# Quantising and the first product by whole batches of 256 tokens, with x1 formed in place

## What is computed

```python
# L0: 8 thresholds, deltas, zero points
gi = sum(abs(x)[..., None] <= thresholds, -1);  idx = min(gi, G - 1)
d, zp = deltas[idx], zero_points[idx]
q = where(gi == G, 0, (clip(round(x / d) + zp, 0, 63) - zp) * d)
x = x + q                                        # x1
x = x + einsum('bsi,boi->bso', x, W1[id_a[b]])   # x2, a 1024 x 1024 matrix per batch
x = x + x @ W2.T + 0.5 * (x @ A[id_b[b]]) @ B_w.T
x = x + ((x @ B3[id_a[b]].T) @ A3[id_a[b]].T)
```

## Time and profile before

| | us |
|---|---|
| median of 3 runs | 483.82 |
| the 3 runs | 483.77, 483.82, 486.87 |
| profiled execution, first to last instruction | 481.9 |

### The profile page before, as it was taken

The page is one execution under the profiler, slowest core; times in us unless marked ns, Lnnn a source line. Parts: engine busy times, 40 slices in busy tenths (PEclk is TensorE's granted clock), DMA queues, the critical chain, the costliest instruction groups (busy, mean ns, idle before and its releaser), DMA issues.

```text
span 481.9 us, 8215 instructions
## 1 busy us (share of the span) xinstructions
PE 464.9 (96%) x3184; PEld 424.7 (88%) x3184; DVE 419.4 (87%) x481; ACT 358.6 (74%) x383; POOL 45.5 (9%) x46
## 2 busy tenths in 40 slices
PE   3999869999999999999999999999999999999997
PEld 3969669898999989898999989898999989898995
DVE  5999999999999899989999899989999899989120
ACT  6979958678877879678877879678887879675011
POOL 1064000200002000200002000210003000100000
PEclk9999989999999999999999999999999999999999
DMA  7997214712335122712335122712335122702002
GB/s 282 407 415 258 113 34 149 294 54 97 131 127 212 44 95 97 294 44 103 131 120 218 44 89 101 294 44 103 131 101 237 44 86 104 294 2 88 1 1 87
DMA packets 17830, 67.07 MB, mean 139 GB/s; under 512 B 2576, under 2 KB 5904, under 8 KB 13712
## 3 DMA queue, kind: packets, MB, share of 16 engines
q1 hardware_dynamic: 17808, 66.81, 37.9%
HBM read 56.84 MB, written 9.96 MB: 139 GB/s over the span
## 4 chain that ended last, share of the span: by engine, by line
PE 90%; ACT 3%; DMA 3%; DVE 2%; issue 1%; POOL 1%; SPq 0%; DVEq 0%
PE x_bank L603 45%; PE acc L628 34%; PE acc L579 3%; PE x_bank L616 3%; PE acc L640 2%; PE acc L638 2%; DMA w1b<-w 2%; DMA rows<-own_rows 1%; ACT mask L344 1%; ACT w2h L400 1%; DVE y L460 1%; PE acc L567 1%; ACT tq L329 1%; PE acc L577 0%; ACT outb L404 0%
## 5 line engine op out<-in xcount | busy, mean ns | idle before, releaser
L603 PEld LDWEIGHTS x_bank<-x,w1b 128*128 128x128 f32 x2048 | 233.2, 193 | 8.2 <-issue 4.9
L603 PE MATMUL x_bank<-x,w1b 128*128 128x128 f32 x2048 | 234.8, 276 | 3.7 <-DVE x L475 3.7
L344 ACT ACTIVATE mask<-absx,negtop 128x1024 bf16<-128x1024 f32 x112 | 128.4, 1146 | 40.3 <-DVE y L460 39.5
L329 ACT ACTIVATE tq<-xin,magic,rdelta 128x1024 f32<-128x1024 f32 x128 | 157.0, 1234 | 0.6 <-DVE yhigh L526 0.3
L460 DVE COPY_PREDICATED y<-mask,uq 128x1024 f32<-128x1024 int16 x112 | 151.1, 1349 | 0.1
L439 DVE TENSOR_SCALAR tq<-tq,par 128x1024 f32<-128x1024 f32 x128 | 99.2, 775 | 3.7 <-DVE y L460 3.1
L448 DVE TENSOR_SCALAR uq<-tq,ylow,yhigh 128x1024 f32<-128x1024 f32 x112 | 92.3, 824 | 0.2 <-DVE y L460 0.2
L628 PE MATMUL acc<-w2h,x2h 128*128 128x512 f32 x256 | 80.9, 393 | 2.0 <-DVE x2l L481 2.0
L628 PE MATMUL acc<-w2h,x2l 128*128 128x512 f32 x256 | 79.9, 390 | 0.0
L628 PE MATMUL acc<-w2l,x2h 128*128 128x512 f32 x256 | 79.2, 390 | 0.0
L295 POOL TENSOR_TENSOR w1b<-w1b,eye 128x256 f32<-128x256 f32 x32 | 36.5, 1140 | 368.9 <-DMA w1b<-w 368.9
(11 more groups left out here) (57 smaller groups left out, 218.9 us busy)
## 6 DMA issues: line engine op xcount, KB each, us to landing
w1b<-w SPq DMA_DIRECT2D x32, 1024.0 KB, 6.7
xin<-x SPq DMA_DIRECT2D x16, 512.0 KB, 3.7
out<-outb SPq DMA_DIRECT2D x14, 512.0 KB, 2.8
w1b<-w2n SPq DMA_DIRECT2D x4, 1024.0 KB, 10.6
ring<-w2t SPq DMA_DIRECT2D x6, 512.0 KB, 6.7
ua<-e_dram SPq DMA_DIRECT2D x16, 128.0 KB, 2.5
ua<-w2t SPq DMA_DIRECT2D x2, 512.0 KB, 7.8
va<-la SPq DMA_DIRECT2D x8, 128.0 KB, 2.7
```

What stands on the lines that cost most here:

```text
L329: nc.scalar.activation(tq[:, n % TQ, :], flat(xin, c % UN), ACT.Identity, bias=magic[:, 0:1], scale=rdelta[:, g:g + 1]).then_inc(t_ready, 1)
L344: nc.scalar.activation(mask[:, n % MK, :], absx[:, :], ACT.Relu, bias=negtop[:, g:g + 1], scale=1.0).then_inc(mask_ready, 1)
L603: last = nc.tensor.matmul(x2_bank[2 * t + i][:, o % HALF * P:(o % HALF + 1) * P], w1b[:, o, at:at + P], x1[:, t, k, :], start=(o % HALF == ...
```

## The change

- **Quantising by batch.** A step is now a batch and a group: 64 steps of 2048 elements per partition in place of 128 of 1024. Each `multiple`, `exceeds`, `value`, `clamp`, `select` and both closing operations have twice the width and half the count. `clamp` writes back into `tq`, and `uq` is gone; a tq buffer is free only when its `select` is done, and there are 3 in place of 4.
- **x1 in place.** `xin` and `x1` become `xs`, two slots of a whole batch; x1 of a batch is written over its x. x(b+2) is loaded when W1 of batch b is done. Batch 0's x comes in two halves of 512 KB, and both come ahead of the tables' inputs; its first |x|, `multiple` and `value` work by halves.
- **W1 with 256 moving columns.** `w1_x1` runs once a batch over both units: 64 products of 256 columns in place of 128 of 128. x2 is rounded and split in two halves of 1024 elements.
- **PE's order.** W1 of the whole batch, with `u_low` of the last batch after three tiles as before; then the products by W2 for k = 0 to 3 of both units; then k = 4 to 7 of unit 0, v_x2, k = 4 to 7 of unit 1. Batch 0 has the same order and waits for each W2 tile as it goes.
- **Places in the lists.** DVE splits the halves of x2 of batch b at steps 4 and 7 of the quantising of batch b + 1 (2 and 5 for batch 0), the second ahead of that step's `select`. W2 is split at steps 8 to 13, after the first batch is closed. SP issues W2 tiles 4 to 7 behind the stores of the tables, and SP's loop is written out.

The diff, cut to its core (declarations, renamed semaphores and the host's layout of x are left out):

```diff
     P = 128
-    B, _, UN, KT, _ = x.shape
-    T = UN * P
+    B, _, KT, T = x.shape
+    UN = T // P
...
     MAGIC = 1.5 * 2.0 ** 23
     PAIRS = OT // 2
     DH = D // 2
     ACCS = 2 * UN
...
+    TQ, MK, ST = 3, 2, 4
     ctx = ExitStack()
     with ctx:
         def sem(name):
             return ctx.enter_context(nc.semaphore(name))
-        def flat(t, c):
...
-        x2l = sb("x2l", [P, UN, KT, P], f32r)
+        def flat(t):
+            return t.rearrange("p k t -> p (k t)")
+        xs = sb("xs", [P, 2, KT, T])
+        x2h = sb("x2h", [P, KT, T], f32r)
+        x2l = sb("x2l", [P, KT, T], f32r)
...
-        uq = sb("uq", [P, 2, CH])
...
+        b3s = flat(xs[:, 1, 0:HALF, :]).rearrange("p (k r) -> p k r", k=KT)
+        gsb = flat(xs[:, 1, HALF:KT, :]).rearrange("p (a k r) -> p a k r", a=NA, k=KT)
...
+        x2p = ctx.enter_context(nc.psum_tensor("x2p", [P, BANKS, 512], f32))
...
+        low_bank = x2p[:, 3, :]
...
-            load_x(0, 0)
+            load_first(0)
             sp.dma_start(par[:, :, :], params[:, :, :]).then_inc(par_in, 16)
+            load_first(1)
...
-            load_x(0, 1)
...
-            sp.wait_ge(x1_ready, 1)
-            load_x(1, 0)
-            load_w2(4)
-            load_w2(5)
             sp.wait_ge(g_out, 16)
+            load_x(1)
...
-            load_w2(6)
-            load_w2(7)
...
+            for k in range(ST, KT):
+                load_w2(k)
             sp.wait_ge(e_out, 16 * EH)
             sp.wait_ge(w2l_ready, ST + 1)
             load_u(a0)
...
+            for b in range(LAST):
                 a, lab = ids_of(b + 1)
-                if not first:
+                if b:
                     store(b - 1, 0)
                     store(b - 1, 1)
-                sp.wait_ge(vl_ready, 2 * (b + 1))
-                load_v(a, lab)
-                sp.wait_ge(x1_ready, UN * b + 2)
-                load_x(b + 1, 1)
                 for j in range(PAIRS):
                     sp.wait_ge(w1_used, PAIRS * b + j + 1)
                     load_w1(a, j)
...
+                    if j == 1:
+                        sp.wait_ge(vl_ready, 2 * (b + 1))
+                        load_v(a, lab)
+                if b + 2 < B:
+                    load_x(b + 2)
+                sp.wait_ge(ul_ready, b + 1)
+                load_u(a)
...
+        DVE_D = 2
+        ACT_G, ACT_E = 5, 6
+        ACT_W2 = (9, 9, 10, 10, 12, 13, 13, 14)
+        DVE_W2 = (8, 8, 9, 9, 11, 12, 12, 13)
+        X2_FIRST, X2_AT = (2, 5), (4, G - 1)
+        V_AT, U_AT = 3, G - 1
+        LOW_AT = G + 1
+        OUT_AT = (G + 4, G + 4, G + 5, G + 5)
+        END = STEPS + 2 * G
...
                 if n >= TQ:
-                    act.wait_ge(clamped, n - TQ + 1)
-                nc.scalar.activation(tq[:, n % TQ, :], flat(xin, c % UN), ACT.Identity, bias=magic[:, 0:1],
+                    act.wait_ge(chosen, n - TQ + 1)
+                nc.scalar.activation(tq[:, n % TQ, :], flat(xs[:, c % 2, :, :]), ACT.Identity, bias=magic[:, 0:1],
                                      scale=rdelta[:, g:g + 1]).then_inc(t_ready, 1)
...
-                    act.wait_ge(abs_ready, c + 1)
                 if n % G:
+                    act.wait_ge(abs_ready, n // G + 2)
                     if n == 1:
...
                     if n > MK:
-                        act.wait_ge(y_ready, selections(n - MK))
+                        act.wait_ge(chosen, n - MK + 1)
...
-            def round_x2(c, i):
-                b, t = divmod(c, UN)
-                if t == 0:
-                    act.wait_ge(bank0_done, 2 * b + i + 1)
...
+            def round_x2(b, i):
+                act.wait_ge(w1_used, PAIRS * b + 2 * i + 2)
+                nc.scalar.activation(flat(x2h[:, i * HALF:(i + 1) * HALF, :]),
+                                     x2p[:, 2 * i:2 * i + 2, :].rearrange("p j n -> p (j n)"), ACT.Copy) \
+                    .then_inc(x2h_ready, 1)
...
             for n in range(END):
+                c, i = divmod(n, G)
+                if i == 0 and 1 <= n <= STEPS:
+                    exceeds(n - 1)
                 if n < STEPS:
                     multiple(n)
...
+                    if i == 1 and c:
+                        absolute(c)
+                    if i:
+                        exceeds(n - 1)
+                tables(n)
...
-                    if s == ACT_V:
+                    s = n - G * (b + 1)
+                    if s == V_AT + 1:
                         round_v(b)
-                    if s in (ACT_U, ACT_U + 1):
-                        round_u(b, s - ACT_U)
-                    if s == ACT_LOW:
+                    for q in range(ACCS):
+                        if s == OUT_AT[q] + 1 and b < LAST:
+                            finish_out(b, q)
+                    if s == U_AT:
+                        round_u(b, 0)
+                        round_u(b, 1)
+                    for h, at in enumerate(X2_AT if b else X2_FIRST):
+                        if s == min(at + 2, G - 1):
+                            round_x2(b, h)
+                    if s == LOW_AT + 1:
                         round_low(b)
-                    for q in range(ACCS):
-                        if s == ACT_OUT[q] and b < LAST:
-                            finish_out(b, q)
-                tables(n)
...
+            def first_value(h):
+                g = group_of(0)
+                dve.wait_ge(t_ready, h + 1)
+                half = tq[:, 0, h * CP:(h + 1) * CP]
+                nc.vector.tensor_scalar(half, half, -MAGIC, par[:, 1, g:g + 1], ALU.add, ALU.mult).then_inc(u_ready, 1)
...
+                dve.wait_ge(u_ready, n + 2)
                 if n % G:
-                    dve.wait_ge(clamped, n + 1)
-                    dve.wait_ge(mask_ready, selections(n))
-                    if n > 1:
-                        dve.wait_ge(y_ready, selections(n - 1))
+                    nc.vector.tensor_scalar(tq[:, n % TQ, :], tq[:, n % TQ, :], ylow[:, g:g + 1], yhigh[:, g:g + 1],
+                                            ALU.max, ALU.min).then_inc(clamped, 1)
+                else:
+                    if n:
+                        dve.wait_ge(x1_ready, n // G)
+                    nc.vector.tensor_scalar(y[:, :], tq[:, n % TQ, :], ylow[:, g:g + 1], yhigh[:, g:g + 1],
+                                            ALU.max, ALU.min).then_inc(chosen, 1)
             def select(n):
...
+                dve.wait_ge(clamped, selections(n))
+                dve.wait_ge(mask_ready, selections(n))
+                dve.wait_ge(chosen, n)
+                nc.vector.copy_predicated(y[:, :], mask[:, n % MK, :].bitcast(i16), tq[:, n % TQ, :]) \
+                    .then_inc(chosen, 1)
+            def close_batch(c):
+                xc = flat(xs[:, c % 2, :, :])
+                dve.wait_ge(chosen, G * c + G)
                 if c == 0:
-                    dve.wait_ge(abs_ready, 1)
-                nc.vector.scalar_tensor_tensor(ycut, absx[:, :], top[:, G - 1:G], y[:, :],
+                    dve.wait_ge(abs_ready, 2)
+                nc.vector.scalar_tensor_tensor(y[:, :], absx[:, :], top[:, G - 1:G], y[:, :],
                                                ALU.is_gt, ALU.mult).then_inc(y_cut, 1)
                 dve.wait_ge(y_cut, c + 1)
...
+                nc.vector.tensor_tensor(xc, xc, y[:, :], ALU.add).then_inc(x1_ready, 1)
...
+            def split_x2(b, i):
+                dve.wait_ge(x2h_ready, 2 * b + i + 1)
+                half = slice(i * HALF, (i + 1) * HALF)
+                nc.vector.tensor_tensor(flat(x2l[:, half, :]), x2p[:, 2 * i:2 * i + 2, :].rearrange("p j n -> p (j n)"),
+                                        flat(x2h[:, half, :]).bitcast(f32), ALU.subtract).then_inc(x2l_ready, 1)
...
+            for h in range(2):
+                dve.wait_ge(x_first[h], 16)
+                half = flat(xs[:, 0, h * HALF:(h + 1) * HALF, :])
+                nc.vector.scalar_tensor_tensor(absx[:, h * CP:(h + 1) * CP], half, -1.0, half,
+                                               ALU.mult, ALU.max).then_inc(abs_ready, 1)
...
+                c, i = divmod(n, G)
+                if n == 0:
+                    first_value(0)
+                    first_value(1)
+                    clamp(0)
+                    value(1)
+                elif n < STEPS:
+                    if i == 0:
+                        value(n)
+                        value(n + 1)
+                    clamp(n)
+                    if 0 < i < G - 1:
+                        value(n + 1)
+                for b in range(B):
+                    if n == G * (b + 1) + G - 1 and X2_AT[1] == G - 1 and b:
+                        split_x2(b, 1)
+                if n < STEPS and i:
+                    select(n)
                 tables(n)
                 for b in range(B):
-                    s = n - PER * b
-                    if s == DVE_V:
+                    s = n - G * (b + 1)
+                    for h, at in enumerate(X2_AT if b else X2_FIRST):
```

(74 more changed lines are left out.)

216 lines of the change are left out of this document (49 added, 167 removed).

## The result

The changed kernel takes 492.1 us, the median of four runs (491.5 to 493.4), against 485.35 for the kernel before in its four (483.77 to 487.44) on the same chip: a ratio of 1.0135, 95% interval 1.0087 to 1.0182. It is slower, by 1.35% in the middle of an interval that begins at 0.9%, and the forecast of 490.8 was 1.3 us short. The profiled execution of the changed kernel spans 490.4 us, where that of before spans 481.9. Most executions of the kernel before take about 484 or about 487 us, and the profiled one is of the shorter kind, so the spans differ by 8.5 us where the medians differ by 6.7.

What follows compares the result with a forecast made beforehand. PE was taken to bound the steady part, DVE's first units the start. Batch 1 at 109, six batches of 53.6 and a last of 58.4 make 489.0; the median stands 1.9 higher, 490.8. Range 484.5 to 498.

Steps and rivals of the forecast that it cites:

- W1 on PE: Each batch's W1 product: 128 records of 256 columns at 218 ns, 28.0 us with transitions, 0.8 us less a batch.
- Quantising on DVE: DVE's steps at double width: 4.75 us against 5.2 for two before; 40.8 us of quantising a batch, 45.3 in all.
- The start: Up to batch 1: x1 of batch 0 at 54, batch 1 at 109 instead of 96.4, 12.6 us lost.
- The sum from 6.0: DVE's batch 0: |x| 2.3, quantising 40.8, mask 0.4 bring 49.5; 4.4 us of waits for ACT make x1 at 54.
- The steady part: Later batches: PE still sets the pace, 53.6 us each; next x1 is ready at 41, 12 us of slack.
- The sum: Whole kernel: 109 + 6 x 53.6 + 58.4 = 489.0, +7.1 on 481.9; with 1.9 for the median, 490.8.
- The first, a start of 104: Start: tables out before ACT needs them, DVE never waits for masks; x1 at 49.5, total 485.8; chance 0.24.
- The second, nothing saved by wide operations: DVE: double width takes double time; x1 at 57.5, batch 1 at 115, total 496.8; chance 0.11.
- The third, no gain at 256 columns: PE's W1: 256 columns gain nothing, 8 batches x 0.8 = 6.4 us back, total 497.2; chance 0.06.
- The fourth, a new wait in the steady part: Steady batches: closing comes over 12 us late; 2 us over PE's pace in 7 batches, 504.8; chance 0.05.
- A: Theory after the result: start pays once as PE awaits DVE's whole batch; wider W1 gives back 1.2 us a batch.

Runs made afterwards that it cites:

- the best full start: Changed kernel with tables copied out later, PE kept busy before batch 0's W1, and ACT rounding x2's half ahead of u: 490.65 us, 1.0118 of the kernel before.

## Why the prediction was right

**W1 on PE: right in kind, too small.** 218 ns a record were foreseen, 216 measured; 0.8 us a batch, 1.2 measured. Of the difference some 0.26 is the record, worth 128 x 2 ns, and 0.1 the small transitions between stretches, which the term kept at 0.1 and which are gone: 10.36 + 17.27 us are 128 records of 215.9. The Trainium skill (TensorE: Matmul & The Clock Gate, Wait — 56ns, not 53.3ns?) would have two passes of 256 columns last, as an estimate, 218.3 ns. The trace differs from that: 216 measured, as if its 2.5 ns were due once a record here and not twice.

**Quantising on DVE: right per operation, too small in sum.** Selects stand 2.39 us apart at best (2.28 foreseen), values 1.20, clamps 1.26. A batch of DVE was foreseen as 45.3 us. The last operations of batches 2 to 4 (DVE; start, us, what) show it:

```profile
158.06 2.29 DVE L474 TENSOR_TENSOR xs<-xs,y 128x2048 f32<-128x2048 f32 x1
...
205.46 2.29 DVE L474 TENSOR_TENSOR xs<-xs,y 128x2048 f32<-128x2048 f32 x1
...
258.70 2.29 DVE L474 TENSOR_TENSOR xs<-xs,y 128x2048 f32<-128x2048 f32 x1
```

From 110.49 (batch 1) to 158.06 are 47.6 us, to the next 47.4, and then 53.2, PE's pace. So a batch costs DVE 47.5: 8 below PE's were foreseen, 5.7 are there. That is enough for the steady part, but it is what makes the lag at the start long.

**The start: the step that was mis-sized.** x1(0) was foreseen at 54 and came at 56.5. The sum from 6.0 lacks the wait for the second half of x (1.6 us); beside GpSimd's diagonals two clamps and two values, of 1.73, 1.75, 1.47 and 1.83 us, took 1.8 us more of DVE's time, from start to start, than the 1.27 and 1.2 of the sum; against that the waits for ACT behind the tables were 3.1 in place of 4.4, and DVE began 0.3 sooner. That makes 1.8 of the 2.5; the other 0.7 are the seven selects, 2.39 in place of 2.28 each. The sum also has ACT's tables too early, at 30.4 and 37: ACT got them at 32.77 and 39.63, since PE's first work began at 10.48, 2.35 later than before where 1.3 were foreseen. That ACT's waits are shorter than foreseen even so is because DVE, being late itself, stood less. PE's W1(0) took 29.3 us, 1.7 over a steady one (2 us foreseen for the clock; the granted clock was 0.50 from 56 to 60). PE was free 53.5 us behind x1(0), foreseen 53.7. x1(1) was foreseen at 109 and came at 112.8, 56.2 behind x1(0) where the sum had 55. So batch 1 began 3.9 us later than the sum had it: 2.5 from batch 0, 1.2 from DVE's second batch, the rest PE's own beginning.

**The steady part: right.** It was said that x1 of the next batch is there 12 us ahead of PE, and that this covers a late x. In the changed kernel x1 of batch 4 is ready at 261.0 and PE takes it at 272.73, 11.7. PE waits for nobody. The run with x 9 us late confirms the cover, and its size is about the 12 us of the prediction, but it isn't that of x1: by the margins left in that run an x may be 9 + 3.2 = 12.2 us late before the split of x2's half 2 is missed (40.4 us into PE's batch), 13.8 before low's (10.4 us into it), and 16.5 before x1 is. The first two stand in DVE's queue behind the next x. That the two figures of 12 agree is luck. A slack must be read for every product of a queue, not for its last.

**The sum.** 490.8 was foreseen (489.0 and 1.9 make 490.9, to be exact), 492.1 measured. The start cost 16.5 in place of 12.6, 3.9 too little; the width and the order gave 8.0 back in place of some 5.6. The two errors have opposite signs, and that the sum came out nearer than its terms is luck.

**The rivals.** The first, a start of 104, fell: batch 1 begins at 112.92, and no edit of the start brought it below 109.6. Its mechanism was tried as well: with the tables taken late DVE waits for no mask, and x1(0) comes at 54.23 and not at 49.5. The second, nothing saved by wide operations, fell: the kernel with operations of 1024 has its batch 1 2.0 us later. The third, no gain at 256 columns, fell by 0.98 us a batch. The fourth, a new wait in the steady part, is not in this kernel; the runs with a late x show what it looks like.

**Why it is slower, then.** Before, PE could begin with the first 128 tokens of a batch while DVE was still at the others. Now DVE must be some half batch (half of its 47.5 us) further ahead at PE's beginning. That is paid once: PE begins W1 20.6 us later (56.60 against 36.01) and has made up 4.1 of it by batch 1. 16.5 us stand against 1.17 a batch: by this sum it would need some 14 batches behind the first to be even, and the kernel has 7. That is worked out; no run had more batches. The experiments show A as far as they go, each with the 1 us or so by which traces of one start differ: with the tables, the clock, and the rounding mended, 2.6 us come back; with most of W2's split left out, 2.2; with both together but for the rounding, 3.3, or by the estimate above some 5.8. Even that start, 107.1, would leave 107.1 - 96.4 - 8.0 = 2.7 us. So no local reason makes up the 16.5. That the unit of work does is read from PE's 17.0 us of waiting for x1(0), and not tested by itself: a narrow batch 0 ahead of wide ones, which would spare the start and keep the width, wasn't tried.

## What to carry to other kernels

Making the unit of work larger saves in every unit and costs once, at the point where the next engine first has to wait for a whole unit; count how often each falls due before choosing the size. Where engines wait for each other, the gain of mending one is what the next leaves of it: 7.5 us less work on DVE gave 2.7, for ACT's list came next, and 1.7 us less on PE gave nothing, for DVE's split did. When a load is moved, ask not only who wants its data, but what stands behind the first user in that engine's queue.

## What the runs showed of the hardware

The cost of a matmul record isn't quite proportional to its columns: fp32, 128 columns 111.7 ns, 256 columns 216, 512 columns 430.

After a short idle time of PE ahead of batch 1 the clock fell in some runs and not in others. It fell behind 2.60 us (PE kept busy ahead of W1: granted clock 0.59 from 111.3 to 115.3, 12.31 us for 48 records), behind 2.88 (x 9 us late) and behind 3.08 (operations of 1024). It did not behind 2.65 (the best full start), 2.82 (tables late), 2.91 (x behind u's load) and 2.85, the changed kernel (1.00 from 113 to 117, 10.62 us). First the run with 2.60, then that with 2.85:

```profile
111.30:115.30 4.00, 4.00 (x11) 3.25 (x12) 4.00 (x4) 3.98 (x4) 0.00 (x0) 0.59 0.00 0
```

```profile
113.00:117.00 4.00, 4.00 (x19) 3.53 (x20) 4.00 (x4) 3.98 (x4) 0.00 (x0) 1.00 0.00 0
```

So a wait of this length costs 0 or 1.7 us beyond itself, and two starts that differ by less than that can't be told apart by one execution. The length of the wait doesn't decide between 2.6 and 2.9 us; what does is open.

GpSimd's work stretches DVE's, and more the longer its instructions are: clamps of 1.34 us took 1.75 beside diagonals of 128 and 256 columns and 3.4 beside subtractions of 1024, and eight columns of DVE took 4.25 in place of 0.12 beside a filling of 6.93.
